# GpSimd's two residual products change places, and the split of the up weights moves behind the z1 remainder

## What is computed

```python
def layer(h, p):
    q = phi(h @ wq + bq); k = phi(h @ wk + bk); v = h @ wv + bv      # phi = elu + 1
    kv = einsum('bshd,bshm->bhdm', k, v)
    z = 1.0 / (einsum('bshd,bhd->bsh', q, k.sum(axis=1)) + 1e-06)
    att = einsum('bshd,bhdm,bsh->bshm', q, kv, z)
    h = h + att @ wo + bo
    h = _ln(h, g1, be1)                                              # h1 -> z1
    y = gelu(h @ w1 + c1) @ w2 + c2
    return _ln(h + y, g2, be2)                                       # h2 -> z
h, _ = lax.scan(layer, x, params)
x + _ln(h, gf, bef) * silu(expert_gate(x))
```

## Time and profile before

| | |
|---|---|
| three runs | 917.62, 918.11, 920.5 us; median 918.11 |
| the profiled execution | 918.29 us, span 916.2 us, mean granted clock 0.983 |
| TensorE | busy 877.0 us, 96% of the span |
| VectorE | 765.4 us, 84% |
| ScalarE | 705.5 us, 77% |
| GpSimd | 241.2 us, 26%, in 272 instructions |
| chain that ended last | PE 78%, DVE 16%, issue 4%, ACT 1% |

### The profile page before, as it was taken

One profiled execution on the slowest core, in us unless ns is written; L12 is line 12 of the kernel. 1 busy time (PEld: TensorE's weight loads), 2 busy tenths in 40 slices (PEclk: granted clock), 3 DMA queues, 4 the chain that ended last, 5 costly groups with the idle time before them and its releaser, 6 DMA issues.

```text
span 916.2 us, 19024 instructions
## 1 busy us (share of the span) xinstructions
PE 877.0 (96%) x5786; PEld 746.0 (81%) x5786; DVE 765.4 (84%) x2737; ACT 705.5 (77%) x1104; POOL 241.2 (26%) x272
## 2 busy tenths in 40 slices
PE   6799999999999999999999999999999999998876
PEld 3588888888888888888888888888888888877664
DVE  7888789787987878788888878878897888899898
ACT  4799887878787887878787788878878787876553
POOL 5222221322232223312232233222223222212103
PEclk9999999999999999999999999999999999999895
DMA  4200100010000100010000100001000000000002
GB/s 130 73 1 17 26 1 22 1 42 1 0 21 0 40 1 20 0 40 0 1 21 0 40 1 19 2 16 25 1 21 0 0 0 1 9 17 1 1 1 92
DMA packets 21888, 16.21 MB, mean 18 GB/s; under 512 B 3920, under 2 KB 17855, under 8 KB 21824
## 3 DMA queue, kind: packets, MB, share of 16 engines
q1 hardware_dynamic: 20960, 14.95, 5.8%
q10 hardware_dynamic: 864, 0.59, 0.2%
HBM read 13.43 MB, written 2.10 MB: 17 GB/s over the span
## 4 chain that ended last, share of the span: by engine, by line
PE 78%; DVE 16%; issue 4%; ACT 1%; DMA 0%; DVEq 0%; ACTq 0%
PE down_ps L753 21%; PE q_ps L703 6%; PE small_ps L692 5%; PE q_ps L685 5%; PE att_ps L722 5%; PE k_ps L679 5%; PE up_ps L747 4%; PE up_ps L745 4%; PE up_ps L746 4%; PE t_ps L729 3%; PE t_ps L669 3%; DVE st L963 2%; PE small_ps L697 2%; PE att_ps L711 1%; PE small_ps L706 1%
## 5 line engine op out<-in xcount | busy, mean ns | idle before, releaser
L753 PEld LDWEIGHTS down_ps<-w_use,hid 128*128 128x128 f32 x2048 | 249.6, 192 | 29.3 <-issue 29.2
L753 PE MATMUL down_ps<-w_use,hid 128*128 128x128 f32 x2048 | 260.4, 275 | 0.0
L1004 POOL TENSOR_TENSOR res_att<-z_tm,g_att 128x512 f32<-128x512 f32 x64 | 81.5, 1273 | 495.9 <-DVE mv L969 495.9
L855 ACT ACTIVATE hid<-up_ps 128x512 f32<-128x512 f32 x192 | 114.9, 599 | 19.9 <-PE up_ps L747 4.3
L963 DVE BATCH_NORM_STATS2 st<-h 128x6 f32<-128x128 f32 x512 | 105.5, 279 | 2.3
L881 ACT ACTIVATE den<-q_ps,den_eps_col 128x512 f32<-128x512 f32 x64 | 43.9, 686 | 59.1 <-PE q_ps L703 59.0
L1011 POOL TENSOR_TENSOR res_ffn<-z_tm,g_ffn 128x512 f32<-128x512 f32 x64 | 81.5, 1273 | 20.7 <-DVE h L958 20.7
L938 ACT ACT_TABLE_LOAD x63 | 80.8, 1283 | 1.1
L745 PE MATMUL up_ps<-z_hi,w_hi 128*128 128x512 f32 x192 | 80.8, 421 | 0.4 <-DVE z_lo L998 0.4
L922 ACT ACT_TABLE_LOAD x62 | 79.5, 1283 | 1.1
L986 DVE TENSOR_SCALAR z_tm<-h,rstd,shift 128x128 f32<-128x128 f32 x256 | 76.3, 360 | 2.3
(11 more groups left out here) (200 smaller groups left out, 1780.1 us busy)
## 6 DMA issues: line engine op xcount, KB each, us to landing
raw_w<-in_L_attn_W SPq DMA_DIRECT2D x15, 256.0 KB, 4.8
out_y<-gate_tm SPq DMA_DIRECT2D x8, 256.0 KB, 2.1
bias_bc<-in_L_attn_c SPq DMA_DIRECT2D x7, 256.0 KB, 4.5
x_tm<-in_L_attn_x SPq DMA_DIRECT2D x3, 512.0 KB, 5.1
raw_g<-in_L_attn_g SPq DMA_DIRECT2D x14, 64.0 KB
x_tm<-in_L_attn_x SPq DMA_DIRECT2D x2, 256.0 KB, 3.2
raw_att<-in_L_attn_Wq SPq DMA_DIRECT2D x7, 64.0 KB, 1.8
raw_att<-in_L_attn_Wk SPq DMA_DIRECT2D x7, 64.0 KB, 1.9
```

What stands on the lines that cost most here:

```text
L753: last = nc.tensor.matmul(down_ps[:, t, :], hid[:, j, t * P:(t + 1) * P], w2_use[:, j, :], start=False, stop=(j == FC - 1 and t == TT - 1))
L855: nc.scalar.activation(hid[:, j, :], up_bank[j], ACT.Gelu).then_inc(s["gelu"], 1)
L1004: nc.gpsimd.tensor_tensor(res_att[:, :, :], z_tm[:, b, :, :], g_att[:, :].unsqueeze(1).to_broadcast([P, TT, D]), ALU.mult).then_inc(s["t2m ...
```

## The change

In each period GpSimd now does res_ffn first; in position 0 row_att, and in position 2 the w2_use copy and row_ffn, stand behind it; the g_ffn copy of position 1 stands between the two products; res_att comes behind these. VectorE's split of the up weights in position 1 moves from behind g_sb to behind the z1 remainder. No instruction is added or removed, no wait is changed, and TensorE, ScalarE and SyncE have the same order as before.

```diff
@@ pool_period @@
             in_use = not isinstance(l, int) or l > 0
+            if is_unit(p - 2):
+                pool_res_ffn(pool, p - 2, (b - 2) % SEQS)
             if b == 0 and is_unit(p) and in_use:
                 pool_row_att(pool, l, True)
+            if b == 1 and is_layer(l) and in_use:
+                pool_g_ffn(pool, l, True)
+                pool.wait_ge(s["gffn_ready"], l + 1)
             if b == 2 and is_unit(p) and in_use:
                 pool_w2(pool, l, True)
             if b == 0 and is_unit(p):
                 pool.wait_ge(s["gatt_ready"], l + 1)
             if is_unit(p):
                 pool_res_att(pool, p, b)
-            if is_unit(p - 2):
-                pool_res_ffn(pool, p - 2, (b - 2) % SEQS)
-            if b == 1 and is_layer(l) and in_use:
-                pool_g_ffn(pool, l, True)
-                pool.wait_ge(s["gffn_ready"], l + 1)
@@ dve_period @@
             if att:
                 dve_g_copy(dve, p)
-            if b == 1 and in_layers(l, 1, L - 1):
-                dve_split_w1(dve, l)
...
             if ln1:
                 dve_z1_lo(dve, p - 1)
+            if b == 1 and in_layers(l, 1, L - 1):
+                dve_split_w1(dve, l)
```

## The result

| | before | changed |
|---|---|---|
| median | 918.47 us (917.62 to 920.5, 4 runs) | 926.11 us (924.85 to 927.18, 4 runs) |
| ratio | | 1.0077, 95% interval 1.0057 to 1.0097 |
| profiled execution | 918.29 us, span 916.2 us | 925.58 us, span 923.5 us |
| mean granted clock | 0.983 | 0.985 |

The changed kernel is 0.8% slower. Two lines of its page: the busy shares, and the chain of work that ended last.

What follows compares the result with a forecast made beforehand. TensorE, busy nearly throughout, bounds the kernel, so only its waits count. 13.9 + 1.0 - 5.7 - 0.8 - 0.8 - 1.6 = +6.0 us gives a 924.1 us median; 0.9 for the clock makes 925.0 us, 8-in-10 range 918.5 to 932.

Steps and rivals of the forecast that it cites:

- wait of down_bias in position 2: TensorE's down_bias waits for row_ffn, queued behind late h2, res_ffn and the copy: 1.98 us in 7 periods, +13.9 us.
- split and res_ffn off blk's path, position 1: Position 1, layers 1 to 7: with the split moved, blk waits for the kv matmul alone, period 12.74 us: -5.7 us.
- m_r in position 0: Position 0 of the loop's five layers: m_r no longer runs beside res_ffn, 0.15 us each, -0.8 us.
- zf in position 6: Position 6: the two zf instructions stood where res_ffn ran; freed, 0.13 x 6, -0.8 us.
- last layer, positions 4 to 7: Periods waiting for VectorE: m_r gives back up to 0.8 us in each of four, half taken, -1.6 us.
- VectorE under the new places of GpSimd: Early res_ffn delays aff_att in position 4; row instructions meet m_r and norm2's neighbour norm1 in position 3, layer 0: +1.0 us.
- the clock: TensorE's longer waits in seven places might bring a half-clock stretch; half of one costing 1.7 us was taken, +0.9 us.
- rival 1: Position 2: row_ffn is still ready before down_bias, so no wait there; 910.2 us, chance 0.07.
- rival 2: Position 2: the split hardly delays h2, filling idle VectorE time; wait costs 0.92 us each, 916.6 us, chance 0.13.
- rival 3: TensorE's clock falls behind most of the seven new waits in position 2, 936 us, chance 0.11.
- Position 4: res_ffn starts 0.1 us before aff_att, which ends 1.0 us later; h1 late but still hidden before att_bias by 0.2 us.
- Rival 4: res_ffn slows the statistics beside it, 0.62 us in each of 60 periods, some 955 us, chance 0.02.

Runs made afterwards that it cites:

- e3_w2_first: The changed kernel with the w2_use copy and row_ffn put back in front of res_ffn in position 2: 918.8 us, ratio 1.0002 to the kernel before.
- e7_row_twice: The changed kernel with row_ffn computed twice in a row in position 2: 946.4 us, ratio 1.0304 to the kernel before.
- e2_order_only: The changed kernel with the split back behind g_sb, so only GpSimd's order is new: 918.9 us, ratio 1.0006 to the kernel before.
- e5: The changed kernel with w2 copy and row_ffn before res_ffn, GpSimd waiting for q_phi before that copy in position 2: 913.0 us, ratio 0.9941 to the kernel before.
- e6: e4_w2_first_split_old with res_att before res_ffn again in position 4 of every layer and position 3 of the last: 910.6 us, ratio 0.9921 to the kernel before.
- e4_w2_first_split_old: The changed kernel with w2 copy and row_ffn before res_ffn in position 2 and the split back behind g_sb: 912.0 us, ratio 0.9924 to the kernel before.
- e1_split_only: The kernel before with only the split moved behind the z1 remainder, GpSimd's order as before: 926.1 us, ratio 1.0082.

## Why the prediction was right, and where it was not

| term | predicted | read from the profiles |
|---|---|---|
| wait of down_bias in position 2 | +13.9 | +13.7 (7 x 1.95) |
| split and res_ffn off blk's path, position 1 | -5.7 | -5.5 |
| m_r in position 0 | -0.8 | -0.7 |
| zf in position 6 | -0.8 | -0.7 |
| last layer, positions 4 to 7 | -1.6 | -1.4 |
| VectorE under the new places of GpSimd | +1.0 | +2.1 |
| the clock | +0.9 | +0.1 |
| all | +6.9 | +7.6 (span +7.3) |

The second column sums the changes of period lengths by position over the layers, between the two profiled executions; the start of the program, ahead of the first period, was 0.3 us shorter. The total came close in part by luck: the VectorE term was 1.1 us too small and the clock term 0.8 us too large. The terms of positions 0 and 6 are read from the rows (m_r takes 0.16 us there now, the two zf 0.35 us each); no run changed one of them alone.

**The wait** was the decisive step and came out piece by piece: h2's end at 1.38 us (forecast 1.37), res_ffn, copy and row_ffn at 4.64 (4.67), down_bias at 4.70 (4.73). TensorE's idle time was 1.69 us and 11.9 us in sum, a little less than the 1.88 and 13 forecast. e3_w2_first shows that the order makes it, e7_row_twice that it grows with GpSimd's chain one to one, and e2_order_only that 7.2 us of it are the split's delay of h2; rival 1 (in time) and rival 2 (h2 hardly later) are both out, and so is rival 3 for this kernel, with one fall in seven.

**The gain of position 1** had the right size, but the prediction put it down to the split's move. e2_order_only gets it without the move. In the changed kernel either edit suffices, and the move then only costs. The prediction worked out the two edits' terms singly and added them; it did not ask what each would do without the other. That hid that the split's move was all loss here: 7.2 us beside the new order, 7.8 without it, 6.8 with the copy first.

**The split alone** was misjudged on the way (912.9 expected, 926.1 measured). The prediction said "GpSimd is idle there, so both instructions run clear": true of the two instructions, and in the changed kernel of those behind them, since the copy had moved away. With the copy in its old place norm2, the next one on VectorE, is pushed under it and under row_ffn. The margin of 0.08 us between q_e and the copy was there to be read.

**Position 4** is the term that was too small. By the prediction h1 would end near 489.97, with att_bias at 490.14, hidden by 0.2 us. res_ffn was expected 0.1 us ahead of aff_att; it is recorded 0.03 us behind, and aff_att was blocked all the same. It did end with res_ffn, but the delay was 1.14 us and not 1.0 (h1 ended at 494.58, 3.07 us into the period, where 2.93 was expected), and of the 0.2 us of margin the signal's 0.06 had not been taken off. So att_bias came 0.05 us late and took 0.50 instead of 0.40 us: the 0.14 us, in five of the six middle layers. In the sixth (layer 2) h2 and h1 ended earlier in the period, h1 at 2.69 us, and position 4 kept its 13.40. The step that failed is a margin of the size of its own error, counted as cover. Layer 0 (+0.64), the last layer's position 3 (+0.56) and position 3 of the others (+0.05 each in four of them) make most of the rest of the 2.1. In "SBUF — State Buffer", section "SBUF: two separate sides", the Trainium skill counts tensor_scalar among the instructions that can take the lock, and the affines are such, of which no row told before; here the trace agrees, with 1408 ns at the median against 346.

**The clock.** One of the seven new waits, the longest with 1.79 us, was followed by a half-clock stretch; those of 1.68 to 1.69 were not. A stretch of 6.83 us before, in the last layer, did not come in this execution. Its share is +1.7 - 1.6. The forecast of half a fall was a guess at a balance, not a reading. What parts the seventh wait from the six is open: it was 0.1 us longer, and stands in another layer; no run varied the one without the other. The length of the wait alone does not decide. In position 7 of the last layer TensorE waits 2.03 to 2.05 us for g_sb in seven of the profiled executions; the clock fell around it in five (e2, e3, e5, e6, e7) and not in two (the changed kernel and e4). e3_w2_first's profiled execution, the slowest of its twelve, had two more stretches in layer 0, behind waits of 1.2 to 1.7 us that the other kernels have too. Shown is that a wait of 3.0 us in the same place is followed by a fall seven times in seven. Several of the other kernels show a stretch in position 7 of the last layer in their one profiled execution (6.83 us in e1_split_only, none in e4_w2_first_split_old), so 1.6 us of a difference between two profiles can be that.

**Rival 4** is out: the statistics took 276 ns at the median before and 277 now, with res_ffn beside them, and h1 681 ns in both.

## What to carry to other kernels

When an instruction moves on one engine, look at the two that follow it for what they will now stand beside on the other engine: 1.1 us of delay cost little in itself here (at most 0.26 us a period), and VectorE lost 1.4 us more as soon as it pushed an SBUF-to-SBUF instruction under a GpSimd one. When two edits of one change aim at the same collision, work out each without the other; the cheaper one may be the whole gain. Before a loader's copy is queued behind work that waits for another engine, add up the chain to its first reader: three links of 0.6 to 1.3 us behind a late h2 were more than 1.8 us of slack.

## What the runs showed of the hardware

- A GpSimd instruction on 2 partitions (row_ffn, 2x512) took 1.25 to 1.28 us, as long as one on 128 partitions (res_ffn, 1.29 us), and blocked VectorE's norm2 until 0.09 us behind its end.
- Blocked beside GpSimd, all from SBUF to SBUF: the cast (0.42 us clear, 1.46 us blocked), norm2 (0.34, 1.45), aff_att (0.35, 1.41), zf (0.35, 1.28) and m_r with its two SBUF inputs (0.16, 0.96). VectorE was the one blocked even where its start is recorded 0.03 us (aff_att) or 0.08 us (norm2) ahead of GpSimd's; at 0.10 us ahead it kept its time and GpSimd's copy took 707 ns instead of 615. Not slowed: h1 and h2, q_phi, the batch norm statistics and aggregates.
- GpSimd's copy started 0.20 us after the end of q_phi, for which it waited (459.68 to 459.88), and res_ffn 0.08 us after the end of h2 (465.39 to 465.47). It had been idle for over 9 us in both cases; what makes the difference is open.
- TensorE's granted clock fell to half for 3.41 us behind a wait of 3.0 us, seven times in seven, once in seven behind one of 1.7 to 1.8 us in the same place, and in five of seven executions around one of 2.0 us in the last layer; a fall of 3.41 us cost about 1.6 us.
